# A reordered opening, one displaced product and a reordered end in a one-core attention kernel

## The chip, the core and the metric

The kernel runs on one core of a Trainium2 chip. The core has TensorE (PE in the profile; its weight loads are PEld), VectorE (DVE), ScalarE (ACT), GpSimd (POOL) and SyncE (SP), which runs a queue of DMAs here. Each engine works through its own list of instructions in order, and an instruction may first wait for a semaphore that another engine or a DMA raises. The metric is the device time of one execution in microseconds (us).

## The reference

A batch of 4 sequences of 512 tokens with 512 channels is normalised and read as 2 sequences of 1024 tokens. The attention is linear, with a decay per head and a state that is carried from block to block; the result goes through an RMS norm and a gate, and is multiplied by the SiLU of a top-8 router's output:

```python
xn = _layernorm(x)
qkv = silu(einsum('bnf,of->bno', xn, w_qkv))            # 16 heads of 128
o_inter = einsum('bhmd,bhde->bhme', qi * q_decay, kv)
qk = einsum('bhmd,bhnd->bhmn', qi, ki) * diag_decay
kv_new = block_decay * kv + einsum('bhmd,bhme->bhde', ki * k_decay, vi)
out = norm_w * (out * rsqrt(mean(out * out) + EPS))
s = einsum('bno,fo->bnf', sigmoid(xn @ w_gate) * out, w_out)
x = x + s * silu(ffn(xn))        # ffn: softmax scores, top 8 of 64, bias gather
```

## The kernel before

**Products.** All large multiplications are split into a high and a low part (XH and XL for the tokens, WH and WL for the weights) and done as three matmuls of 128 x 512 (`mm3`, L165 to L167). A projection by a pair of heads is a Strassen-Winograd scheme of seven products (`product(g, q)`), each of 6 such matmuls; g counts 64 groups of weights (4 in each of 16 cycles: V, the first head's Q and K, gate, the second head's Q and K). The 14 blocks of XH and XL hold the tokens and the sums and differences that the scheme needs. Product (g, q) writes one of four PSUM banks: BA, BD, or one of two called BS.

**Order.** The program is written as calls that append instructions to five lists. After the opening, the loop emits for each g the products (g,6), (g,2), (g,5), (g,7), (g+1,1), (g,4), (g,3), and after the i-th of these the calls that `plan` put in slot 7g + i: scores, states, inter and intra of the attention for a head and batch, weight parts, moves. A product call also emits what ScalarE and VectorE do with its bank, so a call that is planned a slot later stands behind these on their lists too.

**Weights.** `w_sums_first` and `w_sums_then` form four sums of weight blocks on GpSimd (ST). `w_parts(g, which)` copies to WH on ScalarE (L488) and subtracts to WL on GpSimd (L492); part 0 has 512 columns, part 1 has 768, parts 2 and 3 have 256 each.

**Opening.** Four 128-token tiles of batch 0 (in G, list t0) and four of batch 1 (in XR, list t1) are normalised: those of batch 0 on VectorE (L296), those of batch 1 on ScalarE (`first_norm1`, L343), which waits for a bias nb from GpSimd (L332). `first_turn` transposes a tile of batch 0 into a bank (PS, PT, PO, PX for tiles 0 to 3), `first_a` copies it twice on ScalarE (L363, L364) and `first_a_low` makes the low part on VectorE (L371). `first_blocks(t)` makes 18 matmuls of differences of the two batches, `first_mix`, `first_low` and `first_last` turn them into high and low parts. `constants` and `keep_warm` run matmuls on a tile of zeros; each of their 128 x 128 calls is two instructions in the trace. `decays` is one ScalarE exponential for each head (L217), `clear` a matmul of zeros into a BS bank (L245).

**End.** In the last cycle the output projection of batch 1 (`halves`) needs the low gates GL. `squares` adds a square to SS, `rms_in` sums SS on TensorE and gives the scale rr by a power on GpSimd (L973), `finals` multiplies a bank by rr on VectorE (L1033), `final_sum` adds the residual on VectorE or GpSimd (L1040) and sends the tile out.

Of the kernel before, what the change touches and what calls it, by code (L numbers as in the profile page):

```python
# [14 lines left out]
NH = 16  # L15
# [9 lines left out]
WARM = 8  # L25
# [14 lines left out]
def build(nc, x, wp, small, rw, eb, out):  # L40

    with ExitStack() as ctx:
# [118 lines left out]
        def f32(ap):  # L161
            return ap.bitcast(F32)
# [70 lines left out]
        def keep_warm(*tokens):  # L233
            wait("pe", *tokens)

            def pe(e):
                for _ in range(WARM):
                    i = e.matmul(BD[:, 0:128], zero[:, 0:128], zero[:, 0:128], start=True, stop=True)
                return i
            op("pe", pe)  # L240
# [97 lines left out]
        def first_norm1(ts, tiles):  # L338
            wait("act", tk["nb", ts[0]], tk["rs", 0, ts[0], 1])
# [18 lines left out]
        def first_a(t, bank, d):  # L358

            s = slice(t * 128, (t + 1) * 128)  # L360
            a = bank[:, :].rearrange("p (k n) -> p k n", k=4)
            wait("act", d)
            op("act", lambda e: e.activation(XH[:, 0:4, s], a, ACT.Copy))  # L363
            tk["ca", t] = op("act", lambda e: e.activation(  # L364
                Y[:, 0, t, :].rearrange("p (k n) -> p k n", k=4), a, ACT.Copy))
# [31 lines left out]
        def first_mix(t, bank, more, between=()):  # L397
# [10 lines left out]
            for h_ in between:  # L408
                decays(h_, h_ + 1)
# [3 lines left out]
        def first_low(t, bank, more):  # L413
            s, b, m, tt = first_views(t, bank, more)
            wait("dve", tk["hm", t])
            tk["xb0", t] = op("dve", lambda e: e.tensor_tensor(XL[:, 4:8, s], b, f32(XH[:, 4:8, s]), ALU.subtract))
# [720 lines left out]
        def heads_of(c, base):  # L1137

            steps = (k_turn, k_scale, scores, states, inter, intra, gate, gate_high, gate_low)
            for r, s in ((0, base + 7), (1, base + 21)):  # L1140
                for b, o in ((0, (3, 8, 9, 9, 11, 13, 13, 14, 15)), (1, (8, 12, 13, 13, 15, 17, 17, 18, 20))):
                    for f, k in zip(steps, o):
# [3 lines left out]
                        else:  # L1146
                            plan(s + k, f, c, r, b)
# [355 lines left out]
```

How the kernel before makes its waits and increments, by code:

```python
        def op(e, f):  # L142
            s = done[e]
            count[s.name] += 1
            prog[e].append(lambda eng: f(eng).then_inc(s, 1))
            return s, count[s.name]
# [1 line left out]
        def dma(s, f, e="sp"):  # L149
            count[s.name] += 16
            prog[e].append(lambda eng: f(eng).then_inc(s, 16))
            return s, count[s.name]
# [1 line left out]
        def wait(e, *tokens):  # L155
            for t in tokens:
                if t and t[1] > waited[e].get(t[0].name, 0):
                    waited[e][t[0].name] = t[1]
                    prog[e].append(lambda eng, t=t: eng.wait_ge(t[0], t[1]))
```

## Time and profile before

| | us |
|---|---|
| median of 3 runs | 1054.99 (1053.16 to 1055.17) |
| the profiled execution | 1054.37 |
| its span in the trace | 1052.6 |
| TensorE busy | 1039.8 (99%) |
| VectorE, ScalarE, GpSimd busy | 631.0, 599.9, 674.1 |

The page of the profile gives for each engine the busy time over the span. The granted clock is shown as 9 tenths or more in all 40 slices. The time of the profiled execution is 1.8 us above its span; the run's time holds a little more than the trace between its first and last instruction.

### The profile page before, as it was taken

The numbers are of one execution on the slowest core, as the hardware profiler recorded it, in microseconds if no ns is written. First come the engines' busy times: TensorE is split into PE (matmuls) and PEld (weight loads), VectorE is DVE, ScalarE is ACT, GpSimd is POOL, SyncE is SP. The second block draws the span as 40 slices with busy tenths as digits, with TensorE's granted clock in tenths as the row PEclk, the third lists the DMA queues.
The fourth block names the chain that finished last, engine by engine and source line by source line (L and its number), as shares of the span: only waits on it lengthen the run. The fifth ranks groups of instructions, "written<-read, shape, count | busy, mean of one in ns | idle before, by whom it ended". The sixth has DMA issues, their size and how long they took to land.

```text
span 1052.6 us, 15312 instructions
## 1 busy us (share of the span) xinstructions
PE 1039.8 (99%) x5535; PEld 888.0 (84%) x5535; DVE 631.0 (60%) x1049; ACT 599.9 (57%) x1073; POOL 674.1 (64%) x699
## 2 busy tenths in 40 slices
PE   8999999999999999999999999999999999999997
PEld 7788888888888888888888888888888888888886
DVE  6357566664756666656556655756566575555557
ACT  7766556564655656575554554746555455545543
POOL 6876556574766858587575875747557475665715
PEclk9999999999999999999999999999999999999999
DMA  4333223352444445445753553223254251332235
GB/s 156 81 79 88 51 65 95 72 148 73 115 116 131 103 113 142 124 110 131 248 160 110 173 163 74 70 58 72 70 135 112 51 160 45 76 95 56 67 84 200
DMA packets 215724, 112.39 MB, mean 107 GB/s; under 512 B 174944, under 2 KB 189408, under 8 KB 215648
## 3 DMA queue, kind: packets, MB, share of 16 engines
q1 hardware_dynamic: 198304, 59.48, 24.0%
q10 hardware_dynamic: 17344, 51.93, 15.1%
q8 instruction: 44, 0.72, 0.3%
q14 instruction: 32, 0.26, 0.1%
HBM read 66.47 MB, written 15.73 MB: 78 GB/s over the span
## 4 chain that ended last, share of the span: by engine, by line
PE 93%; POOL 2%; ACT 2%; DVE 1%; issue 1%; DMA 0%; SPq 0%; DVEq 0%; POOLq 0%
PE BS L165 8%; PE BS L167 8%; PE BS L166 8%; PE PS L667 5%; PE PO L768 5%; PE BD L165 5%; PE BA L165 5%; PE BD L167 5%; PE BA L167 5%; PE PX L165 5%; PE BD L166 5%; PE BA L166 5%; PE PX L166 5%; PE PX L167 5%; PE PT L732 4%; PE PO L752 4%
## 5 line engine op out<-in xcount | busy, mean ns | idle before, releaser
L492 POOL TENSOR_TENSOR WL<-ST,WH 128x768 fp32r<-128x768 f32 (+1 forms) x128 | 173.9, 1359 | 132.4 <-ACT WH L488 132.3
L492 POOL TENSOR_TENSOR WL<-STG,WH 128x512 fp32r<-128x512 f32 (+1 forms) x128 | 133.4, 1042 | 134.2 <-ACT WH L488 134.2
L165 PE MATMUL BS<-XH,WH 128*128 128x512 f32 x384 | 158.7, 413 | 0.9 <-DVE XL L422 0.5
L167 PE MATMUL BS<-XH,WL 128*128 128x512 f32 x384 | 150.7, 392 | 0.0
L166 PE MATMUL BS<-XL,WH 128*128 128x512 f32 x384 | 150.0, 391 | 0.0
L833 DVE TENSOR_TENSOR Y<-Y,PX 128x512 f32<-128x512 f32 x104 | 71.5, 687 | 119.9 <-PE PX L167 119.4
L791 POOL TENSOR_TENSOR SS<-SS,SQ 128x512 f32<-128x512 f32 x60 | 86.4, 1440 | 31.2 <-ACT SQ L783 31.2
L165 PE MATMUL BA<-XH,WH 128*128 128x512 f32 x256 | 103.1, 403 | 1.0 <-ACT VT L607 1.0
L165 PE MATMUL BD<-XH,WH 128*128 128x512 f32 x256 | 103.3, 403 | 0.1
L167 PE MATMUL BD<-XH,WL 128*128 128x512 f32 x256 | 100.1, 391 | 0.0
L167 PE MATMUL BA<-XH,WL 128*128 128x512 f32 x256 | 100.1, 391 | 0.0
L166 PE MATMUL BD<-XL,WH 128*128 128x512 f32 x256 | 99.9, 390 | 0.0
L166 PE MATMUL BA<-XL,WH 128*128 128x512 f32 x256 | 99.8, 390 | 0.0
L165 PE MATMUL PX<-OH,GH 128*128 128x512 f32 x244 | 97.1, 398 | 0.0
L488 ACT ACTIVATE WH<-ST 128x768 fp32r<-128x768 f32 (+1 forms) x128 | 80.2, 627 | 26.6 <-PE BD L167 15.4
L166 PE MATMUL PX<-OL,GH 128*128 128x512 f32 x244 | 95.1, 390 | 0.0
L167 PE MATMUL PX<-OH,GL 128*128 128x512 f32 x244 | 95.1, 390 | 0.0
L548 ACT ACTIVATE BS<-BA 128x512 f32<-128x512 f32 x64 | 37.2, 582 | 89.4 <-PE BA L167 88.1
L167 PEld LDWEIGHTS BS<-XH,WL 128*128 128x128 f32 x384 | 72.0, 188 | 16.3
L165 PEld LDWEIGHTS BS<-XH,WH 128*128 128x128 f32 x384 | 72.4, 189 | 13.9 <-issue 0.9
L166 PEld LDWEIGHTS BS<-XL,WH 128*128 128x128 f32 x384 | 72.5, 189 | 12.3
L768 PEld LDWEIGHTS PO<-P,V 128*128 128x128 f32 x496 | 64.8, 191 | 4.8
(307 smaller groups left out, 2405.2 us busy)
## 6 DMA issues: line engine op xcount, KB each, us to landing
STG<-in_wp ACTq DMA_DIRECT2D x77, 512.0 KB, 3.8
V<-VB SPq DMA_DIRECT2D x244, 64.0 KB, 2.4
KN<-P SPq DMA_DIRECT2D x236, 48.0 KB, 2.1
XR<-in_x SPq DMA_DIRECT2D x38, 256.0 KB, 3.2
dgd<-XR ACTq DMA_DIRECT2D x16, 256.0 KB, 2.3
dxl<-XR SPq DMA_DIRECT2D x8, 448.0 KB, 3.5
dxh<-WT SPq DMA_DIRECT2D x8, 448.0 KB, 4.6
XH<-dxh ACTq DMA_DIRECT2D x7, 512.0 KB, 6.3
```

The costliest lines, as they stand in the source:

```text
L165: eng.matmul(o, ah, bh, start=first, stop=False, skip_group_check=skip)
L166: eng.matmul(o, ah, bl_, start=False, stop=False, skip_group_check=skip)
L167: return eng.matmul(o, al, bh, start=False, stop=last, skip_group_check=skip)
L488: a = op("act", lambda e, dst=dst, src=src: e.activation(WH[:, u, dst], src, ACT.Copy))
L492: a = op("pool", lambda e, dst=dst, src=src: e.tensor_tensor(WL[:, u, dst], src, f32(WH[:, u, dst]), ALU.subtract))
L548: tk["seed", g] = op("act", lambda e: e.activation(chain[:, :], BA[:, :], ACT.Copy))
L667: m = e.matmul(PS[:, chunk(k)], kk[:, chunk(k)], q[:, chunk(k)], start=(k == 0), stop=True, skip_group_check=True)
L732: m = e.matmul(PT[:, chunk(i)], KD[:, chunk(i)], v[:, i, :], start=True, stop=True)
L752: m = e.matmul(PO[:, chunk(k)], KV[:, k - 1, :], q[:, chunk(k)], start=(k == 1), stop=False, skip_group_check=True)
L768: m = e.matmul(PO[:, chunk(k)], v[:, k, :], P[:, b, chunk(k)], start=False, stop=True, skip_group_check=True)
L791: a = op("pool", lambda e: e.tensor_tensor(SS[:, b, :], SS[:, b, :], SQ[:, :], ALU.add))
L833: a = op("dve", lambda e: e.tensor_tensor(dst, dst, bank[:, :], ALU.add))
```

## The change

On TensorE the opening now has 13 zero matmuls instead of 8 at the start, the clear of a BS bank ahead of the turn of tile 1, 4 zero matmuls after it, the turns of tiles 2 and 3, and then 3 more. A row with x2, x4, ... stands for so many equal ones. Before, on TensorE, from the first matmul on (PS, PT, PO, PX are the banks of the turns of tiles 0 to 3, BS the clear, P the zeros):

```order
L188 MATMUL PX<-P 128x128 x8
L351 MATMUL PS<-ident,G 128x128 x4
L351 MATMUL PT<-ident,G 128x128 x4
L245 MATMUL BS<-P 128x512
L238 MATMUL BD<-P 128x128 x8
L351 MATMUL PO<-ident,G 128x128 x4
L351 MATMUL PX<-ident,G 128x128 x4
L380 MATMUL BD<-ident,XR 128x128 x2
L383 MATMUL BD<-ident,XR 128x128
L384 MATMUL BD<-KD,XR 128x128
L383 MATMUL BD<-ident,XR 128x128
```

And now:

```order
L189 MATMUL PX<-P 128x128 x13
L350 MATMUL PS<-ident,G 128x128 x4
L244 MATMUL BS<-P 128x512
L350 MATMUL PT<-ident,G 128x128 x4
L237 MATMUL BD<-P 128x128 x4
L350 MATMUL PO<-ident,G 128x128 x4
L350 MATMUL PX<-ident,G 128x128 x4
L237 MATMUL BD<-P 128x128 x3
L381 MATMUL BD<-ident,XR 128x128 x2
L384 MATMUL BD<-ident,XR 128x128
L385 MATMUL BD<-KD,XR 128x128
```

Eight zero matmuls between the turns of tiles 1 and 2 have become four, and three stand behind the turn of tile 3.

On ScalarE the norms of batch 1 (XR) stand one by one between the copies, three decays (DQ) stand after the copies of tile 0 and one ahead of those of tile 2, and the weight part of 768 columns (WH<-ST) has gone behind the first copies of the blocks of tile 0 (XH<-BD). Before, ScalarE from the first weight part (WH<-STG) on:

```order
L488 ACTIVATE WH<-STG 128x512
L343 ACTIVATE XR<-XR,TINY,rs 128x512 x2
L363 ACTIVATE XH<-PO 128x4x128
L364 ACTIVATE Y<-PO 128x512
L363 ACTIVATE XH<-PX 128x4x128
L364 ACTIVATE Y<-PX 128x512
L488 ACTIVATE WH<-ST 128x768
L343 ACTIVATE XR<-XR,TINY,rs 128x512 x2
L406 ACTIVATE XH<-BD 128x4x128
L407 ACTIVATE XH<-BS 128x2x128
L411 ACTIVATE XH<-K 128x4x128
```

And now:

```order
L493 ACTIVATE WH<-STG 128x512
L218 ACTIVATE DQ<-DQ,SMALL 128x256
L362 ACTIVATE XH<-PO 128x4x128
L342 ACTIVATE XR<-XR,TINY,rs 128x512
L365 ACTIVATE Y<-PO 128x512
L342 ACTIVATE XR<-XR,TINY,rs 128x512
L362 ACTIVATE XH<-PX 128x4x128
L365 ACTIVATE Y<-PX 128x512
L407 ACTIVATE XH<-BD 128x4x128
L408 ACTIVATE XH<-BS 128x2x128
L493 ACTIVATE WH<-ST 128x768
L342 ACTIVATE XR<-XR,TINY,rs 128x512
```

On GpSimd the weight part WL of 512 columns has moved behind the bias of tiles 2 and 3, one subtraction of the blocks (XL<-K) has gone to VectorE and another (XL<-V, tile 2) has come, and WL of part 3 of the first group stands behind the sums of the second. The second bank of blocks 1 and 3 is PO instead of PX, and tile 3's first is PX instead of PO.

The states of the first head and batch are planned one slot later. TensorE around them before (PS scores, PT states; six rows of BS are one product, and BA begins the next):

```order
L667 MATMUL PS<-Q,K 128x128 x4
L732 MATMUL PT<-V,KD 128x128 x3
L165 MATMUL BS<-XH,WH 128x512
L166 MATMUL BS<-XL,WH 128x512
L167 MATMUL BS<-XH,WL 128x512
L165 MATMUL BS<-XH,WH 128x512
L166 MATMUL BS<-XL,WH 128x512
L167 MATMUL BS<-XH,WL 128x512
L165 MATMUL BA<-XH,WH 128x512
```

And now, in the same place:

```order
L672 MATMUL PS<-Q,K 128x128 x4
L166 MATMUL BS<-XH,WH 128x512
L167 MATMUL BS<-XL,WH 128x512
L168 MATMUL BS<-XH,WL 128x512
L166 MATMUL BS<-XH,WH 128x512
L167 MATMUL BS<-XL,WH 128x512
L168 MATMUL BS<-XH,WL 128x512
L737 MATMUL PT<-V,KD 128x128 x3
L166 MATMUL BA<-XH,WH 128x512
```

The product into BS that stood behind the states stands ahead of them. The VectorE work of that product, an addition to G that waits for a ScalarE copy, thereby stands ahead of the three VectorE steps of the states (KV) too.

At the end GpSimd makes the last squares' sum ahead of the low gate, and the second scale rr ahead of the second residual sum. Before, its last rows:

```order
L791 TENSOR_TENSOR SS<-SS,SQ 128x512 x2
L973 TENSOR_TENSOR rr<-TINY 128x4
L812 TENSOR_TENSOR GL<-G,GH 128x512
L791 TENSOR_TENSOR SS<-SS,SQ 128x512
L1040 TENSOR_TENSOR XR<-XR 128x512 x2
L973 TENSOR_TENSOR rr<-TINY 128x4
L1040 TENSOR_TENSOR Q<-Q 128x512
```

And now:

```order
L796 TENSOR_TENSOR SS<-SS,SQ 128x512 x2
L978 TENSOR_TENSOR rr<-TINY 128x4
L796 TENSOR_TENSOR SS<-SS,SQ 128x512
L817 TENSOR_TENSOR GL<-G,GH 128x512
L1045 TENSOR_TENSOR XR<-XR 128x512
L978 TENSOR_TENSOR rr<-TINY 128x4
L1045 TENSOR_TENSOR XR<-XR 128x512
```

The rows of SS and GL have changed places, and so have the second rr and the second XR.

```diff
-WARM = 8
+WARM = 13
+CALM = 4
...
-        def keep_warm(*tokens):
-            wait("pe", *tokens)
-
-            def pe(e):
-                for _ in range(WARM):
+        def keep_warm(n):
+            def pe(e):
+                for _ in range(n):
...
         def first_norm1(ts, tiles):
-            wait("act", tk["nb", ts[0]], tk["rs", 0, ts[0], 1])
+            wait("act", tk["nb", ts[0] // 2 * 2], tk["rs", 0, ts[0], 1])
...
-        def first_a(t, bank, d):
+        def first_a(t, bank, d, between=()):
...
             op("act", lambda e: e.activation(XH[:, 0:4, s], a, ACT.Copy))
+            for f, *more in between:
+                f(*more)
             tk["ca", t] = op("act", lambda e: e.activation(
...
-        def first_low(t, bank, more):
+        def first_low_b(t, bank, more):
+            s, b, m, tt = first_views(t, bank, more)
+            wait("dve", tk["hb", t])
+            tk["xb0", t] = op("dve", lambda e: e.tensor_tensor(XL[:, 4:8, s], b, f32(XH[:, 4:8, s]), ALU.subtract))
+
+        def first_low_m(t, bank, more):
             s, b, m, tt = first_views(t, bank, more)
             wait("dve", tk["hm", t])
-            tk["xb0", t] = op("dve", lambda e: e.tensor_tensor(XL[:, 4:8, s], b, f32(XH[:, 4:8, s]), ALU.subtract))
             tk["xm0", t] = op("dve", lambda e: e.tensor_tensor(XL[:, 8:10, s], m, f32(XH[:, 8:10, s]), ALU.subtract))
...
-                            plan(s + k, f, c, r, b)
+                            plan(s + k + ((c, r, b) == (0, 0, 0) and f is states), f, c, r, b)
...
             if t == 0:
                 first_stats(0, (2, 3), t0)
                 w_sums_first(0)
+                clear(0, tk["zero"])
             elif t == 1:
                 first_stats(1, (0, 1), t1)
                 w_sums_then(0)
-                clear(0, tk["zero"])
-                keep_warm()
-        for t in range(2):
-            first_a(t, banks0[t], d0[t])
-        w_parts(0, (0,))
-        first_norm1((0, 1), t1)
-        for t in (2, 3):
-            first_a(t, banks0[t], d0[t])
+                keep_warm(CALM)
+        keep_warm(CALM - 1)
+        first_a(0, PS, d0[0])
+        decays(EARLY, EARLY + 3)
         first_a_low(0, PS)
         first_stats(1, (2, 3), t1)
+        first_a(1, PT, d0[1])
+        w_parts(0, (0,))
+        decays(EARLY + 3, EARLY + 4)
+        first_a(2, PO, d0[2], [(first_norm1, (0,), t1)])
+        first_norm1((1,), t1)
+        first_a(3, PX, d0[3])
+        first_a_low(2, PO)
+        first_a_low(1, PT)
+        pairs = ((BD, BS[1]), (PS, PO), (PT, BS[1]), (PX, PO))
+        first_blocks(0, t0, t1, *pairs[0])
+        first_blocks(1, t0, t1, *pairs[1], tk["xa", 0, 0], tk["xa", 0, 2])
+        first_mix(0, *pairs[0], [(w_parts, 0, (1,)), (first_norm1, (2,), t1)])
         first_a_low(3, PX)
-        first_a_low(1, PT)
-        first_a_low(2, PO)
-        w_parts(0, (1,))
-        first_norm1((2, 3), t1)
-        pairs = ((BD, BS[1]), (PS, PX), (PT, BS[1]), (PO, PX))
-        first_blocks(0, t0, t1, *pairs[0])
-        first_blocks(1, t0, t1, *pairs[1], tk["xa", 0, 0], tk["xa", 0, 3])
-        first_mix(0, *pairs[0])
-        decays(EARLY, EARLY + 1)
-        first_low(0, *pairs[0])
-        first_last(0, "pool")
-        first_mix(1, *pairs[1], range(EARLY + 1, EARLY + 2))
+        first_low_b(0, *pairs[0])
+        first_low_m(0, *pairs[0])
+        first_mix(1, *pairs[1], [(first_norm1, (3,), t1)])
+        first_last(0, "dve")
         product(0, 1)
...
+        first_low_m(2, *pairs[2])
+        first_last(2, "pool")
+        first_low_m(3, *pairs[3])
         first_last(3, "dve")
+        first_low_b(3, *pairs[3])
+        product(0, 2)
         clear(1, tk["xm0", 2])
-        w_parts(0, (2, 3))
+        w_parts(0, (2,))
+        w_sums_first(1)
+        decays(EARLY + 4, NH)
+        end_decays()
         w_parts(1, (0,))
-        product(0, 2)
-        w_sums(1)
-        plan(1, decays, EARLY + 5, NH)
-        plan(1, end_decays)
+        w_sums_then(1)
         plan(1, first_out)
+        plan(1, w_parts, 0, (3,))
...
+        gate_high(c, 1, 1)
         gate_low(c, 0, 1, "pool")
-        gate_high(c, 1, 1)
...
+        finals(2, None)
         sums(0, "pool")
+        rms_in(1, PT, 16, (tk["rr", 0],))
         sums(1, "pool")
-        finals(2, None)
-        rms_in(1, PT, 16, (tk["rr", 0],))
         finals(3, "dve")
```

## Rows read from the trace of the kernel before

**Rows 1.** Windows: PE, PEld, DVE, ACT, POOL busy us (x), granted clock, DMA share, GB/s.

```profile
14.40:60.00 45.60, 42.40 (x231) 34.99 (x230) 20.75 (x35) 34.21 (x66) 38.29 (x43) 1.00 0.26 68
60.00:1000.00 940.00, 939.93 (x4999) 803.91 (x4998) 566.90 (x935) 535.54 (x954) 610.49 (x620) 1.00 0.39 104
1000.00:1047.30 47.30, 47.30 (x272) 40.66 (x270) 30.67 (x51) 20.74 (x37) 16.40 (x13) 1.00 0.45 132
```

**Rows 2.** Instructions of lines 188 and 238: duration ns min/median/max, starts, forms.

```profile
L188 PE MATMUL PX<-P x16: 421/421/581, 1.5 to 4.9; 128*128 128x128 f32 x16
...
L238 PE MATMUL BD<-P x16: 274/421/421, 11.7 to 14.7; 128*128 128x128 f32 x16
```

**Rows 3.** Timeline, 3 to 21 us: start, us, engine, line, out<-in, xcount, idle before.

```profile
3.92 3.70 ACT L217 ACTIVATE DQ<-DQ,SMALL 128x256 f32<-128x256 f32 x9 [1.18 <-DMA SMALL<-in_small]
...
10.58 1.48 DVE L296 TENSOR_SCALAR G<-G,mv,rs 128x512 f32<-128x512 f32 x2
...
12.80 1.52 ACT L343 ACTIVATE XR<-XR,TINY,rs 128x512 f32<-128x512 f32 x2 [0.95 <-POOL TINY L332]
...
15.69 0.38 PE L380 MATMUL BD<-ident,XR 128*128 128x128 f32 x2
...
16.90 0.62 ACT L364 ACTIVATE Y<-PX 128x512 f32<-128x512 f32 x1
...
17.38 0.86 ACT L488 ACTIVATE WH<-ST 128x768 fp32r<-128x768 f32 x1
...
17.47 0.39 PE L384 MATMUL BS<-KD,G 128*128 128x128 f32 x2
...
18.32 1.83 POOL L492 TENSOR_TENSOR WL<-ST,WH 128x768 fp32r<-128x768 f32 x1 [1.58 <-ACT WH L488]
...
20.34 0.48 PE L165 MATMUL BA<-XH,WH 128*128 128x512 f32 x1
```

**Rows 4.** Timeline, 21 to 44 us.

```profile
21.58 1.27 POOL L422 TENSOR_TENSOR XL<-K,XH 128x512 fp32r<-128x512 f32 x1 [0.74 <-ACT XH L411]
...
24.62 1.11 POOL L405 TENSOR_TENSOR V<-Y,V 128x256 f32<-128x256 f32 x1 [1.08 <-DVE V L402]
...
29.58 0.47 PE L165 MATMUL BS<-XH,WH 128*128 128x512 f32 x1 [0.49 <-DVE XL L422]
...
29.89 0.74 POOL L492 TENSOR_TENSOR WL<-ST,WH 128x256 fp32r<-128x256 f32 x1 [1.85 <-ACT WH L488]
...
34.88 0.47 PE L165 MATMUL BA<-XH,WH 128*128 128x512 f32 x1 [0.96 <-ACT VT L607]
...
43.10 0.57 ACT L572 ACTIVATE K<-BS 128x512 f32<-128x512 f32 x1
...
43.73 0.50 PE L165 MATMUL BS<-XH,WH 128*128 128x512 f32 x1 [0.40 <-ACT K L572]
```

**Rows 5.** Timeline around the first states, 54 to 59 us.

```profile
54.96 0.94 PE L732 MATMUL PT<-V,KD 128*128 128x128 f32 x6 [0.51 <-ACT KD L704]
...
57.95 0.69 DVE L558 TENSOR_TENSOR G<-G,BD 128x512 f32<-128x512 f32 x1 [0.96 <-ACT G L556]
...
58.50 0.83 PE L752 MATMUL PO<-Q,KV 128*128 128x128 f32 x6
```

**Rows 6.** Timeline of the end, 1038 to 1051 us.

```profile
1037.98 1.30 POOL L812 TENSOR_TENSOR GL<-G,GH 128x512 fp32r<-128x512 f32 x1
...
1039.24 1.30 POOL L791 TENSOR_TENSOR SS<-SS,SQ 128x512 f32<-128x512 f32 x1
...
1042.60 1.42 DVE L1040 TENSOR_TENSOR K<-K 128x512 f32<-128x512 f32 x1
...
1043.43 1.47 POOL L973 TENSOR_TENSOR rr<-TINY 128x4 f32<-128x4 f32 x1
...
1044.99 0.75 DVE L1033 SCALAR_TENSOR_TENSOR STG<-BS,rr,STG 128x512 f32<-128x512 f32 x1 [0.97 <-POOL rr L973]
...
1050.09 0.33 SPq L1042 DMA_DIRECT2D out<-ST  x1
```

More of the change, by code:

```diff
@@ L407, in first_mix @@
             tk["hm", t] = op("act", lambda e: e.activation(XH[:, 8:10, s], m, ACT.Copy))
-            for h_ in between:
-                decays(h_, h_ + 1)
+            for f, *more_ in between:
+                f(*more_)
             wait("act", a)
             tk["ht", t] = op("act", lambda e: e.activation(XH[:, 10:14, s], tt, ACT.Copy))
-        def first_low(t, bank, more):
+        def first_low_b(t, bank, more):
[3 more added lines that the diff above has]
+        def first_low_m(t, bank, more):
             s, b, m, tt = first_views(t, bank, more)
             wait("dve", tk["hm", t])
-            tk["xb0", t] = op("dve", lambda e: e.tensor_tensor(XL[:, 4:8, s], b, f32(XH[:, 4:8, s]), ALU.subtract))
             tk["xm0", t] = op("dve", lambda e: e.tensor_tensor(XL[:, 8:10, s], m, f32(XH[:, 8:10, s]), ALU.subtract))
@@ L1323, in build @@
+        first_a_low(3, PX)
+        first_low_b(0, *pairs[0])
+        first_low_m(0, *pairs[0])
+        first_mix(1, *pairs[1], [(first_norm1, (3,), t1)])
+        first_last(0, "dve")
         product(0, 1)
-        first_low(1, *pairs[1])
+        first_low_b(1, *pairs[1])
+        first_low_m(1, *pairs[1])
         first_blocks(2, t0, t1, *pairs[2], tk["xa", 0, 1], tk["xm0", 0])
-        first_blocks(3, t0, t1, *pairs[3], tk["xa", 0, 2], tk["xm0", 1])
-        first_mix(2, *pairs[2], range(EARLY + 2, EARLY + 3))
+        first_blocks(3, t0, t1, *pairs[3], tk["xa", 0, 3], tk["xm0", 1])
@@ L1328, in build @@
+        first_mix(2, *pairs[2])
         first_last(1, "dve")
-        first_low(2, *pairs[2])
+        first_low_b(2, *pairs[2])
         first_mix(3, *pairs[3])
-        decays(EARLY + 3, EARLY + 5)
-        first_last(2, "dve")
-        first_low(3, *pairs[3])
+        first_low_m(2, *pairs[2])
+        first_last(2, "pool")
+        first_low_m(3, *pairs[3])
         first_last(3, "dve")
+        first_low_b(3, *pairs[3])
+        product(0, 2)
         clear(1, tk["xm0", 2])
-        w_parts(0, (2, 3))
+        w_parts(0, (2,))
@@ L1337, in build @@
+        w_sums_first(1)
+        decays(EARLY + 4, NH)
+        end_decays()
         w_parts(1, (0,))
-        product(0, 2)
-        w_sums(1)
-        plan(1, decays, EARLY + 5, NH)
-        plan(1, end_decays)
+        w_sums_then(1)
         plan(1, first_out)
+        plan(1, w_parts, 0, (3,))
         plan(2, w_parts, 1, (1,))
         at[3].insert(0, (w_parts, (1, (2, 3))))
-        tk["bd_free"], tk["ps"], tk["pt"], tk["po"], tk["px"] = (
+        tk["bd_free"], tk["ps"], tk["pt"], tk["px"], tk["po"] = (
```

## The prediction

> **What bounds the kernel now.** I read the windows of the whole span first. From 60 to 1000 us TensorE is busy for 939.93 of 940 us, and from 1000 to 1047.30 for all of it [rows 1]. Nothing that the other engines do there can be seen in the time. TensorE gives time away in three places only: before and in the opening (42.40 busy of 45.60 us from 14.4 to 60 us, and more ahead of that), and behind its last matmul at 47.30 of the last stretch, where the tail to the last output DMA at 1050.09 follows [rows 1, 6]. The timeline of these places came next, since the sum is made of moments: when TensorE begins each piece, and what released it. A piece that starts x us sooner on TensorE moves everything behind it by x, until the next wait that does not move with it.
>
> **The opening, up to the first product.** The norms of batch 1 can't begin before 12.80, when GpSimd's bias comes [rows 3]. What stands ahead of that bias on VectorE and GpSimd isn't moved, so 12.80 stays. In the kernel before TensorE began the blocks of tile 0 only at 15.69 [rows 3]: it was in the zero matmuls and the turns of tiles 2 and 3, whose zero matmuls ran to about 15.0 (the last start of line 238 is 14.7) [rows 2]. With four of them instead of eight, the turn of tile 2 follows its norm, and those of both tiles end at 12.06 (10.58 + 1.48) [rows 3]; both turns are then done by about 12.6.
>
> Does ScalarE reach the first norm by 12.80? Its nine decays end at 7.62 (3.92 + 3.70), 0.41 each. Between them and the norm it now has five copies of 0.48 (16.90 to 17.38), one weight part of 512 columns (under the 0.86 of 768 columns, say 0.63), and four decays: 2.40 + 0.63 + 1.64 = 4.67 us in 5.18 [rows 3]. It does, with 0.5 to spare. From 12.80: norm 0.76 (half of 1.52), copy, norm, two copies: 13.56, 14.04, 14.80, 15.76.
>
> The blocks of a tile take 2.0 us (15.69 to 17.69, where the last pair begins at 17.47 and runs at 0.11 each) [rows 3]. Tile 0: 13.65 to 15.65. Tile 1 (its norm is done at 14.85): to 17.65. Product (0,1) starts at 17.7 instead of 20.34 [rows 3].
>
> **The opening, up to the second group.** ScalarE's copies of blocks 0 begin when the blocks have landed (15.8) and VectorE has made its addition (0.4): 16.3. Then 0.5 + 0.3 of copies, the weight part of 768 columns (0.75), norm 0.76, copy 0.6, copies 0.8, norm 0.76: the last norm ends at 20.8. Blocks 2 run from 19.1 (17.7 + 1.4 for a product) to 21.1, blocks 3 to 23.1; here TensorE is the slower one. The last high parts need the addition (23.7), GpSimd's subtraction (1.11: 24.8) and the copy (25.5). GpSimd then has the low part of tile 2 (1.27: about 26.1), VectorE that of tile 3 (26.15) [rows 4]. Product (0,6), which waits for both, starts at 26.25 instead of 29.58. The clear that stood ahead of product (0,2) is behind it now and fits in that gap.
>
> Three products took 34.88 - 0.96 - 29.58 = 4.34 us, so product (1,1) could start at 30.6, where it waits for a ScalarE copy. The table load and that copy end at 30.3, because the last decays were taken out from in front of them: the wait of 0.96 [rows 4] goes, and TensorE is 4.3 us ahead. What is late next is GpSimd. From 29.89 on it worked without a pause towards the sums of the third group [rows 4]; the same pieces (one in another place) now begin behind the low part of tile 2, at 26.1. The copy K<-BS at 43.10 stands behind these sums on ScalarE, and product (1,7) at 43.73 behind that copy [rows 4]. They move by 29.89 - 26.15 = 3.7, not 4.3. A subtraction of 256 columns took GpSimd 1.11 at 24.62 and 0.74 at 29.89 [rows 4], and XL<-K of tile 0 now runs on VectorE beside GpSimd's 1.83 us part; I take 0.2 off. Opening: **-3.5**. Its bounds: -4.3 if GpSimd catches up, -2.5 if GpSimd pays 0.4 in two or three places more.
> The Trainium skill (GPSIMD Engine Reference, Key points) says that GpSimd shares its SBUF interfaces with VectorE and suffers beside an instruction with two SBUF inputs. The trace agrees in 1.11 against 0.74; by the rule the move of XL<-K to VectorE is a loss and not a gain, and the sum would stand at -3.1 rather than -3.5.
>
> **TensorE's clock.** Line 238's matmuls lasted 421 ns up to shortly before the end and 274 ns then; those of line 188 421 or more [rows 2]. So in this trace the clock was at its lower level (1.2 GHz) until about 14.3 and at 2.4 GHz since, though the granted clock reads 1.00, and it rose in the stretch of unbroken work that began at 9 to 10 us. Now TensorE works unbroken from 1.51: 26 zero matmuls, 0.21 apart while it is at the lower level, end at 7.3, next to the first turn. If the clock rises there, turns and clear are out of ScalarE's way. If it doesn't, the clear of 1.7 us ahead of the turn of tile 1 brings ScalarE about 0.7 late to its first norm. That is inside the bound of -2.5.
>
> **First states.** They waited 0.51 for KD at 54.96 [rows 5]. Now the BS product starts at 54.45 instead and ends at 55.85, the states at 56.5. But VectorE's addition for that product, which came 0.83 behind its end (57.12, then 57.95 [rows 5]), now stands ahead of the KV steps: 56.7 to 57.3. The KV steps take about 1 us (an estimate: a product of 1.4 us hid them, as inter at 58.50 did not wait [rows 5]): 58.3. Inter starts at 58.4 instead of 58.50. The wait changes its place: **-0.1**, bounds -0.5 (VectorE quicker) and +0.4.
>
> **The end.** VectorE's last scalings waited for the second rr: 43.43 + 1.47 = 44.90, start 44.99 [rows 6]. Now the squares' sum takes the place at 37.98 and the low gate runs to 40.54. TensorE needs it for its last 24 matmuls, 0.235 apart back from 47.30 [rows 1]: at 41.6, so 1.1 us of cover; a later gate would cost one for one. The sum for rms is done early, but its matmuls stand where they stood on TensorE. GpSimd does one XR sum to 42.0, then rr to 43.5 at the latest. VectorE is now held by its own sum of K, 42.60 + 1.42 = 44.02 [rows 6]. The scalings start at 44.05: -0.94, and what is behind them stays as long (5.10 to 50.09). Taken **-0.9**. Bounds: -1.3, since the last matmul at 47.30 leaves a scaling (0.75) and a sum (0.7) behind it; -0.3, if the displaced XR sum slows VectorE's last sums, as 1.42 for K shows.
>
> **Sum.** -3.5 - 0.1 - 0.9 = -4.5. From the profiled execution, 1054.37 (span 1052.6), this is 1049.9; the median of the runs stands 0.6 above that execution, so 1050.5. All bounds together give -6.1 to -2.4.
>
> **Rivals.**
> 1. GpSimd and VectorE slow each other through the opening, and the wait at product (1,7) grows: opening -2.5, 1051.5. For it: GpSimd has 38.29 us of work in 45.60 [rows 1] and no slack where (1,7) waits. Against: most moves keep its list's length.
> 2. The gain of the opening is hidden anyway, by a GpSimd backlog that doesn't move and is met behind 44 us: only the end's 0.9 is left, 1054.1. For it: as in 1. Against: TensorE lost only 0.51 us between 44 and 60 and 0.07 behind 60 [rows 1, 5].
> 3. Slower: with fewer zero matmuls TensorE idles for shares of 8.4 to 13.6 us, the clock falls to 1.2 GHz ahead of the blocks and doesn't rise while they come with pauses. Each 1 us of work then costs 0.5 more than at 2.4 GHz (421 against 274 ns for one, twice the pitch). Until 30 us that is about 15 us of work, 7.5 us lost: 1057.8. It decides for slower once more than 9 us are spent so. Against it: in the kernel before the clock kept up through the 0.96 us before 34.88 [rows 4]. If it rises again in 5 us of unbroken work, as before, the loss is 2.5: 1053.0. The Trainium skill (TensorE: Matmul & The Clock Gate, What's actually happening) has the lower level as the default and activity as what lifts it, which would make this the danger of fewer zero matmuls; no row here shows a fall.
>
> **Chances.** Forecast 0.64, rival 1 0.20, rival 2 0.08, rival 3 0.08 in all, half of it slower. A measurement of this kernel tells about 0.2% (2.1 us) from no change. Faster by over that (below 1052.9): 0.64 + 0.20 + a little of the rest, 0.87. Same: 0.09. Slower: 0.04. The range holds forecast and rival 1 with the bounds: 1049.0 to 1052.8.
>
> **What would show it.** Blocks of tile 0 at 13.65 and product (0,1) at 17.7; (0,6) at 26.3; (1,1) without a wait; a wait of some 0.6 at (1,7), near 40.1; states without a wait and inter with one; rr ahead of 43.5 and the first of the last scalings at 44.05, less the 3.6 of the opening. The zero matmuls of the opening's second half at 274 ns. It is wrong if TensorE shows waits behind 60 us, if (1,7) moves by less than 2.5 us, or if the low gate holds the last 24 matmuls.

## The result, and the profile after

The changed kernel took 1050.37 us (median, 1050.24 to 1051.39), the kernel before 1055.08 beside it. The ratio is 0.9959, 95% interval 0.9946 to 0.9972: faster by 3.0 to 5.7 us. The profiled execution took 1050.29 with a span of 1048.6, against 1054.37 and 1052.6: 4.08 less.

Windows of the changed kernel, in the columns of [rows 1]. They are set 3.8 and 4.0 us ahead of those, a little more than TensorE itself moved (3.3 to 3.4 us from product (1,7) on), so they hold nearly the same work:

```profile
10.60:56.20 45.60, 42.05 (x230) 34.68 (x231) 25.32 (x44) 35.80 (x68) 41.93 (x49) 1.00 0.34 93
...
56.20:996.00 939.80, 939.73 (x4998) 804.36 (x4997) 567.26 (x934) 535.06 (x953) 611.43 (x621) 1.00 0.39 104
...
996.00:1043.30 47.30, 47.30 (x272) 40.84 (x271) 30.86 (x52) 20.95 (x37) 16.22 (x14) 1.00 0.43 130
```

As in [rows 1], TensorE is idle for only 0.07 us of the long middle. What was gained is gained at the two ends. The moments, with the prediction's beside them:

| start of | before | predicted | after | moved |
|---|---|---|---|---|
| blocks of tile 0 | 15.69 | 13.65 | 13.64 | -2.05 |
| product (0,1) | 20.34 | 17.7 | 17.62 | -2.72 |
| product (0,6) | 29.58 | 26.25 | 26.91 | -2.67 |
| product (1,1) | 34.88 | 30.6 | 31.23 | -3.65 |
| product (1,7) | 43.73 | 40.1 | 40.40 | -3.33 |
| inter | 58.50 | 54.9 | 55.08 | -3.42 |
| last output DMA | 1050.09 | 1045.6 | 1046.01 | -4.08 |

GpSimd's bias for the first norm of batch 1 (L332 before, L331 after), ahead of everything that the change touches, ended at 12.77 before and 12.65 after, and 12.46 to 12.80 in the other traces. So 0.12 of each "moved" is not the change's: counted from the bias, product (1,7) came 3.21 sooner.

The timeline of the changed kernel's opening (start, us, engine, line, out<-in, xcount, idle before and its releaser), the answer to [rows 3, 4]:

```profile
13.64 0.44 PE L381 MATMUL BD<-ident,XR 128*128 128x128 f32 x2 [0.32 <-ACT XR L342]
...
17.62 0.47 PE L166 MATMUL BA<-XH,WH 128*128 128x512 f32 x1
...
18.04 1.84 POOL L497 TENSOR_TENSOR WL<-ST,WH 128x768 fp32r<-128x768 f32 x1 [0.56 <-ACT WH L493]
...
19.22 1.21 DVE L427 TENSOR_TENSOR XL<-K,XH 128x512 fp32r<-128x512 f32 x1 [0.87 <-ACT XH L412]
...
19.84 1.18 POOL L406 TENSOR_TENSOR K<-Y,K 128x256 f32<-128x256 f32 x1
...
24.24 0.74 POOL L406 TENSOR_TENSOR V<-Y,V 128x256 f32<-128x256 f32 x1 [1.25 <-DVE V L403]
...
24.94 1.27 POOL L427 TENSOR_TENSOR XL<-V,XH 128x512 fp32r<-128x512 f32 x1
...
25.68 1.09 DVE L427 TENSOR_TENSOR XL<-V,XH 128x512 fp32r<-128x512 f32 x1
...
26.18 1.18 POOL L497 TENSOR_TENSOR WL<-ST,WH 128x256 fp32r<-128x256 f32 x1
...
26.91 0.47 PE L166 MATMUL BS<-XH,WH 128*128 128x512 f32 x1 [0.96 <-DVE XL L427]
...
31.23 0.47 PE L166 MATMUL BA<-XH,WH 128*128 128x512 f32 x1
...
39.77 0.57 ACT L577 ACTIVATE K<-BS 128x512 f32<-128x512 f32 x1
...
40.40 0.50 PE L166 MATMUL BS<-XH,WH 128*128 128x512 f32 x1 [0.55 <-ACT K L577]
```

Product (1,1) has no idle time in front of it any more, and the wait at (1,7) has grown from 0.40 to 0.55. Two VectorE subtractions of 512 columns took 1.21 and 1.09, each beside GpSimd at work. Around the states, as [rows 5]:

```profile
52.33 0.83 PE L737 MATMUL PT<-V,KD 128*128 128x128 f32 x6
...
53.37 0.69 DVE L563 TENSOR_TENSOR G<-G,BD 128x512 f32<-128x512 f32 x1 [1.52 <-ACT G L561]
...
54.29 0.73 DVE L745 SCALAR_TENSOR_TENSOR KV<-KV,DQ,PT 128x128 f32<-128x128 f32 x2
...
55.08 0.94 PE L757 MATMUL PO<-Q,KV 128*128 128x128 f32 x6 [0.53 <-DVE KV L745]
```

The states wait no more; inter waits 0.53 for KV, which stands behind the addition to G. The end, as [rows 6]:

```profile
1038.81 1.01 POOL L978 TENSOR_TENSOR rr<-TINY 128x4 f32<-128x4 f32 x1
...
1039.24 0.69 DVE L1045 TENSOR_TENSOR K<-K 128x512 f32<-128x512 f32 x1
...
1039.99 0.75 DVE L1038 SCALAR_TENSOR_TENSOR STG<-BS,rr,STG 128x512 f32<-128x512 f32 x1
...
1041.35 0.75 DVE L1038 SCALAR_TENSOR_TENSOR STG<-BD,rr,STG 128x512 f32<-128x512 f32 x1 [0.60 <-PE BD L168]
...
1046.01 0.33 SPq L1047 DMA_DIRECT2D out<-ST  x1
```

The second rr took 1.01 instead of 1.47 and VectorE's sum of K 0.69 instead of 1.42. The first of the last scalings starts 5.00 us sooner than in [rows 6], so 1.66 more than TensorE moved (3.34), but the second then waits 0.60 for TensorE's bank.

### The profile page after: what moved, and what is told of

Read it like the earlier page. It is cut to its first block, busy times and chain, and to the rows that moved or that the text cites. A ratio compares the mean times of both kernels' runs of the same rounds, so it can differ in the third digit from the quotient of the medians.

```text
span 1048.6 us, 15330 instructions
## 1 busy us (share of the span) xinstructions
PE 1038.6 (99%) x5543; PEld 887.7 (85%) x5543; DVE 632.6 (60%) x1049; ACT 599.4 (57%) x1073; POOL 675.2 (64%) x699
## 4 chain that ended last, share of the span: by engine, by line
PE 94%; POOL 3%; DVE 1%; ACT 1%; issue 0%; DMA 0%; ACTq 0%; DVEq 0%; POOLq 0%
PE BS L166 8%; PE BS L168 8%; PE BS L167 8%; PE PO L773 5%; PE BD L166 5%; PE BD L168 5%; PE PS L672 5%; PE BD L167 5%; PE PX L166 5%; PE BA L166 5%; PE BA L168 5%; PE BA L167 5%; PE PX L167 5%; PE PX L168 5%; PE PO L757 4%; PE PT L737 4%
```

## The experiments

Edits are against the changed kernel unless they say otherwise. Times are medians in us, and ratios are against the kernel before, run beside, with 95% intervals. That kernel's own median was 1055.0 beside experiments 1 to 4 and 1054.1 to 1054.3 beside 5 to 12, so times of different experiments compare only through the ratios, and their intervals, 2 to 3 us wide, overlap with that of the change (0.9946 to 0.9972) in all but experiments 1 and 10. What an edit of half a us does is read from its trace.

Moments in different traces carry the shift of the bias. Inside the opening I therefore count from the start of the blocks of tile 0. In the changed kernel product (0,6) starts 13.27 behind it and (1,7) 26.76; in the traces of experiments 2, 3, 7, 9 and 12, which leave this stretch as it is, 13.27 to 13.29 and 26.74 to 26.78. From (1,7) to the last matmul, chance waits and edited waits taken off, the traces differ by up to 0.7 us, with no idle time of TensorE to show for it.

**1. The end alone.** On the kernel before:

```diff
+        gate_high(c, 1, 1)
         gate_low(c, 0, 1, "pool")
-        gate_high(c, 1, 1)
...
+        finals(2, None)
         sums(0, "pool")
+        rms_in(1, PT, 16, (tk["rr", 0],))
         sums(1, "pool")
-        finals(2, None)
-        rms_in(1, PT, 16, (tk["rr", 0],))
```

> The kernel before with the two moves at the end alone (the last squares' sum ahead of the low gate, the second rr ahead of the second residual sum). My theory: the opening stays as it was and the last matmul at 1047.3; rr ends near 1043.1 instead of 1044.9, the first of the last scalings starts 1.6 us sooner, but the second waits for TensorE's bank, so the last output DMA starts 0.75 us sooner (1049.3): 1054.3 beside a kernel before of 1055.0. Rival 1: the end is worth nothing by itself, since its gain came only with the sooner opening: last output DMA at 1050.1. Rival 2: VectorE's sum of K stays at 1.42 us and holds the scalings: they start at 1044.05, gain 0.94 at that point.

1053.65 against 1055.03, ratio 0.9990 (0.9981 to 0.9999). Its trace holds one wait that has nothing to do with the edit, 1.2 us near 464 us, so the end is read from its own last matmul. The first three rows are from its timeline, the last from the list of TensorE's waits (us, times, longest):

```profile
1043.63 0.69 DVE L1040 TENSOR_TENSOR K<-K 128x512 f32<-128x512 f32 x1
...
1045.73 0.75 DVE L1033 SCALAR_TENSOR_TENSOR STG<-BD,rr,STG 128x512 f32<-128x512 f32 x1 [0.60 <-PE BD L167]
...
1050.40 0.33 SPq L1042 DMA_DIRECT2D out<-ST  x1
...
PE BD L165 <- DVE K L563: 1.2, 1, 1.2
```

The last matmul ended at 1048.35 and the DMA started 2.05 behind it; in the kernel before these were 1047.30 and 2.79. The end is worth 0.74 by itself, and the scaling's wait of 0.60 for TensorE is there too. The first rival falls by the 0.74, the second by K's sum, which took 0.69.

**2. States in their old slot.**

```diff
-                            plan(s + k + ((c, r, b) == (0, 0, 0) and f is states), f, c, r, b)
+                            plan(s + k, f, c, r, b)
```

> The changed kernel with the states of the first head and batch put back to their old slot. My theory: the states wait about 0.5 us for KD again, and the wait of 0.53 in front of inter is gone; inter starts at 55.1 within 0.15 and the time is the same as the changed kernel's (1050.4) within 0.3. Rival: the displaced states are worth the 0.5 us of the wait that they removed: inter at 55.6, time 0.5 longer.

1051.67, ratio 0.9968 (0.9955 to 0.9980). Five runs between 1050.20 and 1052.09 are too few and too spread to tell 0.1 from 0.5 us, and the median was not within 0.3 of the changed kernel's. The trace, which also holds a chance wait of 0.41 at 524.92, tells it: the states wait 0.53 for KD at 51.52, nothing waits at inter (55.06). Inter starts 14.79 behind (1,7), in the changed kernel 14.68. So a wait of 0.53 stands in place of one of 0.53, and the move is worth 0.11. As expected in kind; the time is inconclusive.

**3. The opening alone.** The changed kernel with the states in their old slot, as in 2, and the end in its old order, the edit of 1 reversed.

> The changed kernel with states and end as they were before: the opening alone. My theory: product (1,7) starts at 40.4 and inter near 55.1, everything behind is 3.3 us sooner, the last matmul ends at 1044.0, the last output DMA starts at 1046.8: 1051.2 beside 1055.0. Rival: the pieces do not add, part of the opening's gain is lost at the end where the old order waits for rr: 1052 or more.

1051.33, ratio 0.9969 (0.9960 to 0.9979): 2.2 to 4.2 us. Product (1,7) at 40.41, last matmul end at 1044.19, last DMA:

```profile
1039.53 1.39 DVE L1045 TENSOR_TENSOR K<-K 128x512 f32<-128x512 f32 x1
...
1040.33 1.47 POOL L978 TENSOR_TENSOR rr<-TINY 128x4 f32<-128x4 f32 x1
...
1046.99 0.33 SPq L1047 DMA_DIRECT2D out<-ST  x1
```

The DMA stands 2.80 behind the last matmul as in the kernel before (2.79), with the 1.47 of rr and 1.39 of K's sum back. It came 3.10 sooner than in the kernel before. With the end's 0.74 and the states' 0.09 that makes 3.93 of the 4.08; the 0.15 left is within what traces differ by.

**4. A part of GpSimd's backlog on VectorE.** In `w_parts`, with the release of the buffer widened to all its readers:

```diff
-                wait("pool", a)
-                a = op("pool", lambda e, dst=dst, src=src: e.tensor_tensor(
+                en = "dve" if (g, i) == (0, 3) else "pool"
+                wait(en, a)
+                a = op(en, lambda e, dst=dst, src=src: e.tensor_tensor(
```

> The changed kernel with one GpSimd subtraction (the weight part of 256 columns, part 3 of the first group, 0.74 us at 31.66) given to VectorE, which is idle there. My theory: the wait of 0.55 in front of product (1,7) is GpSimd's backlog (its sums of the third group end at 38.6 and release ScalarE): these sums end 0.7 us sooner, the wait goes, product (1,7) starts at 39.85 and the time falls by 0.5 us, if VectorE's part beside GpSimd does not cost as much as it saves (then 0.3). Rival: the wait comes from ScalarE's own list: product (1,7) stays at 40.4.

1050.63, ratio 0.9962 (0.9949 to 0.9974), and (1,7) moved by 0.15, not 0.55:

```profile
32.20 2.55 POOL L498 TENSOR_TENSOR WL<-ST,WH 128x768 fp32r<-128x768 f32 x2 [0.51 <-ACT WH L493]
...
40.25 0.50 PE L166 MATMUL BS<-XH,WH 128*128 128x512 f32 x1 [0.42 <-ACT K L578]
```

GpSimd, rid of 0.74 us, ran into a wait of 0.51 for ScalarE's copy of the part of 768 columns (31.28 to 32.12). That copy stands behind ScalarE's table load (29.19) and its copy VT<-BS (28.57), which waits for product (0,6). So GpSimd's list is the bound by a hair only: with 0.15 less of it, the bound is product (0,6) itself through ScalarE. My theory held for 0.15 us.

**5. XL<-K of tile 0 back on GpSimd.**

```diff
-        first_last(0, "dve")
+        first_last(0, "pool")
```

> The changed kernel with the subtraction XL<-K of tile 0 back on GpSimd, as before the change. My theory: on VectorE it took 1.21 us beside GpSimd's part of 768 columns, and 0.68 alone; on GpSimd it takes 1.27 and pushes GpSimd's later pieces, K<-Y,K of tile 1 first, by up to 1.2: product (0,6) starts at 27.5 or later instead of 26.91, (1,7) at 41.0 instead of 40.40, time 0.5 longer than the changed kernel. Rival (the rule on shared interfaces): without the contention the opening gets quicker, (0,6) at 26.5.

My theory was wrong and the rival right. The runs, 1049.85 (1049.79 to 1050.98), ratio 0.9965 (0.9953 to 0.9977), do not tell it, but the trace does:

```profile
19.72 0.74 POOL L406 TENSOR_TENSOR K<-Y,K 128x256 f32<-128x256 f32 x1
...
20.41 1.28 POOL L427 TENSOR_TENSOR XL<-K,XH 128x512 fp32r<-128x512 f32 x1
...
26.36 0.47 PE L166 MATMUL BS<-XH,WH 128*128 128x512 f32 x1 [0.96 <-DVE XL L427]
```

Product (0,6) starts 0.55 sooner and (1,7) at 39.83, 0.57 sooner. The blocks of tile 0, which the edit does not touch, began at 13.51 instead of 13.64; counted from them it is 0.42 and 0.44. K<-Y,K takes 0.74 instead of 1.18 and runs ahead of XL<-K on GpSimd, so nothing is pushed. The move to VectorE, a part of the change, cost 0.4 us.

**6. No zero matmuls behind the turns of tiles 1 and 3.**

```diff
-                keep_warm(CALM)
-        keep_warm(CALM - 1)
```

> The changed kernel without the 4 zero matmuls behind the turn of tile 1 and the 3 behind the turn of tile 3 (the 13 at the start stay). My theory: the clock, up since 7.5, stays at 2.4 GHz over the idle stretches between 9.4 and 13.6 us, and the product matmuls start at the same moments: (0,6) at 26.91, time 1050.4. Rival (the prediction's third): the clock falls to 1.2 GHz; the blocks of tile 0, 2.0 us long, take up to 4, and the time grows by 2 us or more.

Wrong again: 1051.82, ratio 0.9980 (0.9971 to 0.9989). Windows of this kernel (the granted clock is the third number from the end) around the blocks of tile 0, and of the changed kernel:

```profile
9.00:13.50 4.50, 1.70 (x12) 1.19 (x13) 4.46 (x11) 4.50 (x11) 4.15 (x8) 1.00 0.95 356
...
13.50:17.10 3.60, 3.60 (x18) 3.60 (x19) 1.72 (x6) 2.11 (x4) 2.82 (x5) 0.55 0.00 0
```

```profile
9.00:13.60 4.60, 3.30 (x27) 2.88 (x26) 4.57 (x10) 4.60 (x11) 4.13 (x8) 1.00 1.01 366
...
13.60:15.70 2.10, 2.06 (x18) 2.06 (x19) 1.76 (x6) 2.10 (x4) 1.83 (x5) 1.00 0.15 42
```

After a stretch in which TensorE was busy for 1.70 of 4.50 us instead of 3.30 of 4.60, the clock was at 1.2 GHz (0.55 over the window) for the blocks of tile 0, and these took 3.63 us instead of 2.06. It was back at 2.4 GHz from about 17.1 on. Product (0,6) came at 28.39, 1.48 later, and 1.62 later counted from the blocks' start. The prediction's third rival is a real mechanism, for 1.6 us, and the seven zero matmuls keep it away. The clock seems not to fall in every execution: eight of the ten runs have a mean granted clock of 0.996 to 0.998 and took 1051.4 to 1053.4, and the two with 1.000 took 1050.5, no longer than the changed kernel. Only one of the eight has a trace.

**7 and 12. Eight zero matmuls at the start, twice.**

```diff
-WARM = 13
+WARM = 8
```

> The changed kernel with 8 zero matmuls at the start instead of 13, as before the change. My theory: the clock is still at 1.2 GHz at the turn of tile 0 and at the clear, the turn of tile 1 and the four zero matmuls behind it take twice as long, and it rises between 11 and 15 us, so that the blocks of tile 0 begin at 13.65 but end up to 2 us late: time 0 to 2 us longer. Rival: the zero matmuls at the start have no effect and everything stands where it stood, (0,6) at 26.91.

> The changed kernel with 8 zero matmuls at the start once more. In its first trace the clock was up at the turn of tile 0 (6.87), while the kernel before, with the same 8, had it down until 14.3. My theory: when it rises is a matter of the single execution; with 8 a trace with a late rise (after 9 us) is possible, and then the blocks of tile 0 end up to 2 us late. Rival: with the turns and the clear at their new places the rise comes early every time: turn of tile 0 at 272 ns again, (0,6) at 26.7, and the times lie within 1 us of the changed kernel's.

1050.84 and 1050.41, ratios 0.9970 (0.9958 to 0.9982) and 0.9969 (0.9958 to 0.9980). The turn of tile 0 (duration ns min/median/max, starts) in the first trace and in the second:

```profile
L350 PE MATMUL PS<-ident,G x4: 272/272/299, 6.9 to 7.2; 128*128 128x128 f32 x4
```

```profile
L350 PE MATMUL PS<-ident,G x4: 421/421/447, 6.9 to 7.6; 128*128 128x128 f32 x4
```

The same kernel has the clock up at 6.9 us in one execution and down until the turn of tile 1 (9.5 to 10.1) in the other, and product (0,6) at 26.69 and 26.97. Of these 0.28 us the bias explains 0.07 (it ended at 12.46 and 12.53). The other 0.2 is the late clock: ScalarE began its first norm 0.08 behind the bias in the first trace and 0.29 behind it in the second. So the second theory held, with 0.2 us and not up to 2.

What the 13 zero matmuls do show is when the clock rises. With 13, the turn of tile 0 ran at 272 ns in all ten traces; with 8, in one of four (this first one; the second, the kernel before and experiment 1 have 421). They spare a risk of 0.2 us, too little for the medians.

**8. XL<-V of tile 2 on VectorE.**

```diff
-        first_last(2, "pool")
+        first_last(2, "dve")
```

The call's place is as it was, only its engine changes: on VectorE it stands behind XL<-BS and ahead of XL<-PO.

> The changed kernel with the subtraction XL<-V of tile 2 (1.27 us on GpSimd at 24.94) on VectorE too, ahead of that of tile 3. My theory: product (0,6) waits 0.96 for VectorE's XL<-V of tile 3, which takes 1.09 only because GpSimd's of tile 2 runs beside it. Both on VectorE, 0.68 each: (0,6) at 26.4, and GpSimd is rid of 1.27 us, so (1,7) starts 0.5 sooner, at 39.9; time 0.5 shorter than the changed kernel. Rival: VectorE has no room, its list ends later than 26.77 and (0,6) moves back.

1049.99, ratio 0.9962 (0.9950 to 0.9975). Product (0,6) at 26.53, (1,7) at 40.01: 0.38 and 0.39 sooner, and 0.29 and 0.30 counted from the blocks of tile 0 (13.55). Right in kind. VectorE's first subtraction took 1.12, not 0.68, beside GpSimd's subtraction V<-Y,V, and its second took 0.68. GpSimd, rid of 1.27 us, was not 1.27 sooner:

```profile
25.95 1.03 POOL L497 TENSOR_TENSOR WL<-ST,WH 128x256 fp32r<-128x256 f32 x1 [1.04 <-ACT WH L493]
```

It waited 1.04 for ScalarE's copy and began this part only 0.23 sooner (26.18 in the changed kernel).

**9. Inter one slot later too.**

```diff
-                            plan(s + k + ((c, r, b) == (0, 0, 0) and f is states), f, c, r, b)
+                            plan(s + k + ((c, r, b) == (0, 0, 0) and f in (states, inter)), f, c, r, b)
```

> The changed kernel with inter of the first head and batch one slot later too, so that a product stands between the states' last VectorE step and inter. My theory: the states move only displaced the wait, since VectorE's addition for the product now stands ahead of the KV steps; with inter behind one more product the wait of 0.53 in front of it goes and nothing takes its place: the last output DMA starts 0.5 us sooner than the changed kernel's 1046.01, time 0.5 shorter. Rival: what follows inter (its scaling on VectorE, then intra one product on) becomes the wait, and the time stays.

1049.49 (1049.29 to 1050.56), ratio 0.9955 (0.9943 to 0.9968). In its timeline

```profile
54.16 0.73 DVE L745 SCALAR_TENSOR_TENSOR KV<-KV,DQ,PT 128x128 f32<-128x128 f32 x2
...
55.67 0.83 PE L757 MATMUL PO<-Q,KV 128*128 128x128 f32 x6
```

KV ends at 54.89 and inter starts at 55.67 without a wait. The last DMA starts at 1045.21, 0.80 sooner; 0.13 of it was there at (1,7) already, 0.53 is the wait, and 0.14 stays unexplained. The ratio alone does not tell this kernel from the changed one (0.9959).

**10. TensorE's part of the opening alone.** The kernel before with

```diff
-WARM = 8
+WARM = 13
+CALM = 4
...
+                clear(0, tk["zero"])
...
-                clear(0, tk["zero"])
-                keep_warm()
+                keep_warm(CALM)
+        keep_warm(CALM - 1)
```

> The kernel before with TensorE's part of the opening alone: 13, 4 and 3 zero matmuls at their new places and the clear ahead of the turn of tile 1; ScalarE's, VectorE's and GpSimd's lists as before. My theory: ScalarE does the copies of tile 2 right behind both norms (14.3 instead of 15.45), everything to product (0,6) moves by 1.1 us (28.4 to 28.5), and since ScalarE's decays still stand ahead of the table load, the wait at (1,1) stays about 1 us: (1,7) near 42.6, time 1.1 shorter than the kernel before. The other 2.2 us of the opening are the other lists' moves. Rival: the turns are all of it, (1,7) near 40.4 and 3.3 shorter.

1053.37, ratio 0.9993 (0.9984 to 1.0002): by the runs alone it could be no gain at all. The moments are as expected:

```profile
14.26 0.57 ACT L362 ACTIVATE XH<-PO 128x512 fp32r<-128x512 f32 x1
...
16.32 0.69 DVE L370 TENSOR_TENSOR XL<-PX,XH 128x512 fp32r<-128x512 f32 x1 [2.00 <-ACT Y L363]
...
17.16 0.41 PE L379 MATMUL PS<-ident,XR 128*128 128x128 f32 x2 [1.24 <-ACT WH L487]
...
28.39 0.47 PE L166 MATMUL BS<-XH,WH 128*128 128x512 f32 x1 [0.49 <-DVE XL L421]
...
33.70 0.47 PE L166 MATMUL BA<-XH,WH 128*128 128x512 f32 x1 [0.97 <-ACT VT L606]
...
42.52 0.50 PE L166 MATMUL BS<-XH,WH 128*128 128x512 f32 x1 [0.39 <-ACT K L571]
```

The blocks of tile 0 began at 13.70, but those of tile 1 waited 1.24 us. The profile names ScalarE's WH; the program lets them wait for VectorE's XL<-PX, which ended at 17.01 and had itself waited for ScalarE's last copy, behind both norms. The wait of 0.97 at (1,1) stayed. Of the opening's 3.2 us (counted from the bias, which ended at 12.80 here) 1.2 are TensorE's list; 2.0 are the other lists' moves.

**11. Three edits together**: those of 5, 8 and 9.

> The changed kernel with three edits: XL<-K of tile 0 on GpSimd (it moved (0,6) by -0.55 alone), XL<-V of tile 2 on VectorE (-0.38 alone), inter of the first head and batch one slot later (-0.5 expected). My theory: each takes away a wait or a contention of its own, so they add: product (0,6) at 26.0, (1,7) at 39.5, the last output DMA at 1044.6, time 1.4 us shorter than the changed kernel, 1048.9 at the changed kernel's 1050.3. Rival: the first two remove the same contention on the way to (0,6), so only -0.55 of them is left, and the time is 1049.3.

1049.56 (1048.52 to 1050.45), ratio 0.9952 (0.9938 to 0.9965). Product (0,6) at 26.11 and (1,7) at 39.59:

```profile
26.11 0.47 PE L166 MATMUL BS<-XH,WH 128*128 128x512 f32 x1 [0.66 <-DVE XL L427]
...
39.59 0.50 PE L166 MATMUL BS<-XH,WH 128*128 128x512 f32 x1 [0.57 <-ACT K L577]
```

Counted from the blocks of tile 0 (13.58), the edits of 5 and 8 give 0.74 and 0.75 together, and 0.42 + 0.29 and 0.44 + 0.30 apart: they add, and the rival falls. Its last DMA started at 1045.51, not at 1044.6; 0.62 of that is a chance wait at 741.01, the other 0.3 is within what traces differ by. It has the lowest ratio of the study, but its interval overlaps experiment 9's and the changed kernel's.

## Why the prediction was right

**What bounds the kernel.** Right. TensorE's start of each piece moved, the middle passed the shift on (0.07 us idle before and after), and rival 2 fell by that.

**The opening: -3.5 predicted, -3.33 measured** (-3.21 counted from the bias). The steps up to product (0,1) are right within 0.1 us. From there, sizes were off. Product (0,6) came at 26.91 instead of 26.25: VectorE's two subtractions with both operands in SBUF took 1.21 and 1.09, where I had put 0.65, and GpSimd's K<-Y,K 1.18 beside the first. I had charged 0.2 to GpSimd for that move and nothing to VectorE; experiment 5 put the move's price at 0.4. The rule that the prediction set beside its sum was right that the move is a loss, and about its size; the opening as a whole came out between the two sums, 0.17 from the forecast and 0.23 from the rule's -3.1. The Trainium skill (GPSIMD Engine Reference, Key points) gives the rule: the two engines share SBUF interfaces, and a VectorE instruction with two SBUF inputs contends. Experiments 5 and 8 agree, with 1.18 against 0.74 for one subtraction on GpSimd and 1.12 against 0.68 on VectorE.

Half of the miss had no effect at (1,7), because GpSimd began its weight parts at 26.18, as worked out (26.1), and (1,7) hung on it. That agreement was partly luck: VectorE's addition ahead of it ended at 24.16 and not at 23.7, and GpSimd's subtraction at 24.24 took 0.74 and not 1.11. From 26.18 on, 0.38 were lost to (1,7), where I had charged 0.2; the part at 26.18 alone took 1.18 beside VectorE's subtraction, and 0.74 at 29.89 in [rows 4]. The prediction named GpSimd's list as the only bound there; experiment 4 showed that ScalarE's chain from product (0,6) follows only 0.15 us behind.

**Rival 1** named the same contention with 1.0 us. It is real, but the trace shows 0.4 for the one move that brought it in and 0.2 more at (1,7) than charged.

**First states: -0.1 predicted, -0.09 measured.** The wait moved to inter as worked out, and for the reason given: experiments 2 and 9 show 0.53 at either place, and none where inter goes along.

**The end: -0.9 predicted, -0.74 measured.** The step "VectorE is now held by its own sum of K, 42.60 + 1.42" failed. K's sum took 1.42 only because GpSimd added a residual beside it; with rr there instead it took 0.69. The scalings could start 1.66 us sooner, and then TensorE's second bank held them by 0.60, a bound that I had placed at the last matmul only. Two errors in one term nearly cancelled: that -0.74 lies so near to -0.9 is partly luck.

**The clock.** The bound for a late rise was too careful: 0.2 us instead of 0.7 (experiment 12). The third rival had a twelfth of the chance and did not come true, since the zero matmuls that were left sufficed. The argument against it, that the clock kept up through 0.96 us of idleness, was weak: experiment 6 had idle stretches of 1.75 and 1.05 us, and it fell. But it cost 1.6 us and not 7.5, since it was back after 3.6 us. (The rival's 1057.8 should read 1058.0 by its own terms.)

**Sum.** -4.5 predicted, -4.08 between the profiled executions, -4.71 between the medians. The interval of the ratio is wider than these differ, so the runs confirm the sum only to within 1 to 2 us; its terms rest on the traces.

## What to carry to other kernels

When one engine is busy for 99% of the span, walk its list and its releasers' lists from fixed moments, and ask of each wait that goes which list stands 0.2 us behind it. A duration that a row gives holds for what ran beside it on the other engine: 1.42 us became 0.69 when its neighbour changed, and the pairing below says what it becomes. A wait that is removed by putting work between can return one step later, if that work brings its own steps on another engine's list; move the next consumer along.

## What the runs showed of the hardware that was not expected

- The granted clock reads 1.00 in the windows at the start (1.5 to 6.0 us in the kernel before), where matmuls of 128 columns last 421 ns and not 274; it reads 0.55 where it falls later (experiment 6). Durations show both.
- When the clock rises at the start differs between executions of one kernel (by 6.9 us or after 9.5, experiments 7 and 12), and so between the kernels' single traces. In experiment 7 it rose over an idle stretch of TensorE of 1.59 us: its last matmuls before it lasted 421 ns, the first behind it 272. That doesn't explain the spread of the times: the late rise cost 0.2.
- Where a VectorE and a GpSimd instruction that slow each other overlap, the later one ends about its own duration behind the earlier one's end, less 0.13 us. In the changed kernel, XL<-K on VectorE: 19.88 + 0.68 - 0.13 = 20.43, measured 20.43; XL<-V on VectorE: 26.21 + 0.68 - 0.13 = 26.76, measured 26.77. K<-Y,K on GpSimd: 20.43 + 0.74 - 0.13 = 21.04, measured 21.02. In the kernel before, K's sum: 43.47 + 0.69 - 0.13 = 44.03, measured 44.02; rr behind it: 44.02 + 1.01 - 0.13 = 44.90, measured 44.90. The VectorE step of each pair has both operands in SBUF; XL<-PX, with one in PSUM, kept its 0.68 beside GpSimd at 26.69. This is an estimate from these rows, but with it [rows 4, 6] would have given the sizes that the prediction missed.
- Five of the 14 traces hold one chance wait of TensorE of 0.4 to 1.2 us between 100 and 760 us. Neither the trace of before nor that of after has one. Two, 463.69 in experiment 1 and 459.94 in experiment 5, are at the same place of the program, and are this contention decided the other way. First experiment 1, then the changed kernel:

```profile
460.79 2.25 DVE L1098 TENSOR_TENSOR XR<-XR,WT 128x896 fp32r<-128x896 f32 x1 [2.60 <-ACT WT L1094]
...
460.80 1.29 POOL L791 TENSOR_TENSOR SS<-SS,SQ 128x512 f32<-128x512 f32 x1
```

```profile
457.58 2.24 POOL L796 TENSOR_TENSOR SS<-SS,SQ 128x512 f32<-128x512 f32 x1
...
457.59 1.09 DVE L1103 TENSOR_TENSOR XR<-XR,WT 128x896 fp32r<-128x896 f32 x1 [2.59 <-ACT WT L1099]
```

In all 14 traces the two start within 0.01 us of each other. In twelve GpSimd is held and nothing waits; in these two VectorE is held, its addition to K behind it comes 1.2 later, and TensorE waits 1.23 for it. The other three begin with a transfer of V<-VB that comes late. In experiment 2 the states wait 0.41 for it. In experiments 10 (106.99) and 11 (741.01) VectorE waits 0.49 and 0.47 for it and so meets a GpSimd subtraction of 768 columns that it otherwise precedes:

```profile
103.08 1.82 DVE L936 CAST LG<-SC 128x256 fp32r<-128x256 f32 x1
```

This cast took 0.29 or 0.30 at both places in every other trace, and TensorE then waits 0.63 and 0.62. Why the transfer is late was not looked into. These waits are as large as the effects studied here, so these were read from moments ahead of them.
